# A recommendation-layer kernel on one core: x W as the first of ten equal passes, x*x times q as the last, two groups without the seven-product scheme, and the sums of x on VectorE

## The chip, the core and the metric

One NeuronCore of a Trainium2 chip runs the kernel. Its engines work in parallel, each through its own instruction list in order: TensorE (PE; PEld is its weight load), VectorE (DVE), ScalarE (ACT), GpSimd (POOL), and SyncE (SP), which here issues every DMA. Semaphores tie them together. The metric is device time in microseconds (us), less is better. The kernel before takes 815.57 us, the median of three runs (814.37 to 816.1).

## What is computed

```python
# x (2048, 512), beta (1024, 8, 512), W (1024, 512), b (1024)
s   = einsum('bn,hln->bhl', x, beta)
ssq = einsum('bn,hln->bhl', x * x, beta * beta)
y   = 0.5 * sum(s * s - ssq, axis=-1) + x @ W.T + b      # (2048, 1024), float32
```

Since the sum over l can be taken first, the part with ssq is (x*x) times q, with q[n, h] = -0.5 * sum over l of beta squared. So there are three products with the 512 columns n as inner dimension: x beta (8192 columns), x W (1024 columns) and (x*x) q (1024 columns).

## The kernel before

**Groups and passes.** The 2048 rows of x are cut into 8 pairs of 2 x 128 rows. The 8192 columns of beta are cut into 8 passes of 2 x 512 columns. A group is one pair in one pass: a 2 x 2 block product whose inner dimension is cut in two halves of 256 (two steps k of 128). It is done with seven block products instead of eight (Strassen and Winograd's scheme): the sums S1 to S4 of blocks of x, the sums T1 to T4 of blocks of beta, and seven sums behind the products. Each product is made in split single precision: a high part (a cast to fp32r) and a low part (the rest), and three matmuls high*high, high*low, low*high for each k. So a group is 7 x 2 x 3 = 42 matmuls of 128 x 128 by 128 x 512, and 64 groups are 2688.

**Who does what in a group g of the main passes.** PE writes the seven products into four PSUM banks (A, B, E, D; two sets in turn). ACT copies three first products out (`r1`, `r7`, `r5`, lines 549 to 563), and squares the results (lines 543, 569, 573). DVE adds r2 (L750), c12 (L729) and c21 (L721) and sums each eight squares (L738, two per group). POOL adds r5 + r7 (L902) and c22 (L909). The sums over l are stored to `fm_kept` in HBM by SP. The blocks of beta of the next pass are prepared meanwhile in seven steps: T sums on POOL, casts on ACT (L488), the low parts on DVE (L658), beta squared on ACT and its sum over l on DVE (L667, for q).

**The blocks of x.** In pass 0 SP loads each pair, POOL makes the sums S1 to S4 (lines 853 to 861), ACT casts the seven blocks (L538), DVE makes the low parts (L707), SP stores both to HBM. Later passes load them from there; four pairs have room in SBUF.

**The start.** Groups 0 and 1 are made together, product by product, in the order in which their operands come.

**The end.** After the 64 groups come 8 linear groups of 84 matmuls: x W and (x*x) q are added up in the same banks. x*x is made on DVE (L713) and q's blocks are loaded again from HBM, summed, cast and split between the last main group and the first linear one. Each linear group loads `fm_kept`, halves it and adds the bias (L823), adds the products on DVE and POOL, and stores the output. In all PE makes 2688 + 672 = 3360 matmuls, beside 10 to warm up.

The order of the work is written out by hand: every engine has one list, and nothing reorders it.

Of the kernel before, what the change touches and what calls it, by code (L numbers as in the profile page):

```python
# [31 lines left out]

W_PASS, Q_PASS = PASSES, PASSES + 1
SPLIT_FIRST = [B11, B21, T1, T3, B22, T2, T4]
SPLIT_LATER = [T3, B11, T1, B22, T2, B21, T4]
SPLIT_Q = [B11, T1, T3, T2, B21, B22, T4]
SUM_ORDER = [T3, T1, T2, T4]
SUM_ORDER_Q = [T1, T2, T3, T4]


def pairs_of(number):

    if number % 2 == 0:
# [12 lines left out]


def squares_in(i):

    return {1: [0], 2: [1, 2], 3: [3]}.get(i, [])  # L60


def t_split_place(c, op, k=KP - 1):

    if c == 0:
        return 1 + k if op == B11 else SPLIT_FIRST.index(op) + 2
    if c == Q_PASS:
        return 8 + OPS * (c - 1) + SPLIT_Q.index(op) + 1
    return 8 + OPS * (c - 1) + SPLIT_LATER.index(op) + 1


def t_sum_place(c, op):

    if c == 0:
        return {T2: 1, T4: 2}[op]
    return 2 + 4 * (c - 1) + (SUM_ORDER_Q if c == Q_PASS else SUM_ORDER).index(op) + 1


def s_split_place(p, rest=True):

    if p < 2:
        return p + (3 if rest else 1)
    return p + 3


def group_before(g):

    return {1: 0, 2: 1}.get(g, g)


def slot_of(l):

    return (3, 0) if l % 2 == 0 else (2, 1)


def fm_layer(nc, x_p, beta_p, w_p, bias, out):
# [10 lines left out]
    fm_kept = nc.dram_tensor("fm_kept", [B, H], f32, kind="Internal").ap()  # L107

    with ExitStack() as ctx:
# [7 lines left out]
        with ExitStack() as early:  # L117
            def early_sb(name, shape):
                return early.enter_context(nc.sbuf_tensor(name, shape, f32))

            t_hi_in = early_sb("t_hi_in", [P, 2, OPS, KP, COLS])
            t_lo_in = early_sb("t_lo_in", [P, 2, OPS, KP, COLS])
            s_hi_in = early_sb("s_hi_in", [P, HALF, OPS, 256])
            s_lo_in = early_sb("s_lo_in", [P, HALF, OPS, 256])
# [28 lines left out]
        q_loaded = sem("q_loaded")  # L153
# [3 lines left out]
        fm_stored = sem("fm_stored")  # L157
        fm_loaded = [sem(f"fm_loaded{i}") for i in range(2)]
# [3 lines left out]
        x_scaled = sem("x_scaled")  # L162
# [46 lines left out]


        def r1(g):
            return q_in[:, 0, 0, :] if g == 1 else r1_main[:, :]

        def r2(g):
            return q_in[:, 1, 0, :] if g == 1 else r2_main[:, :]

        def r5(g):
            return q_in[:, 2, 0, :] if g == 1 else r5_main[:, :]

        def r7(g):  # L220
            return q_in[:, 3, 0, :] if g == 1 else r7_main[:, :]

        def x_at(p):

            if p < 2:
                return s_hi_in[:, HALF - 1 - p, :, :]
            return s_lo_in[:, p % HALF if p < PAIRS else slot_of(p - PAIRS)[1], :, :]

        def x_loads(p):

            return 16 * (p // HALF + (p % HALF >= 2)) if p < PAIRS else 16 * (2 + (p - PAIRS) // 2)

        def t_at(c, op):

            if c == 0:
                return ub[:, :, :] if op == T1 else t_hi_in[:, 1, op, :, :]
            if c == Q_PASS and op in (B11, B21, B22):
                return q_in[:, op, :, :]
            return t_lo_in[:, c % 2, op, :, :]

        def f_at(l):
            if l % 2 == 0:
                return sq[:, :, :, :].rearrange("p r c h -> p r (c h)")
            return q_in[:, 0:2, :, :].rearrange("p r c h -> p r (c h)")

        @block.sync
        def _(sp):
            def load_first(op, k, loaded):

                ks = slice(0, KP) if k is None else slice(k, k + 1)  # L250
                sp.dma_start(t_hi_in[:, 1, op, ks, :], beta_p[0][:, op, ks, :]).then_inc(loaded, 16)

            def load_blocks(c):
                source = w_p if c == W_PASS else beta_p[c]
                sp.dma_start(t_lo_in[:, c % 2, 0:2, :, :], source[:, 0:2, :, :]).then_inc(right_loaded, 16)
                sp.dma_start(t_lo_in[:, c % 2, 2:4, :, :], source[:, 2:4, :, :]).then_inc(left_loaded, 16)
# [731 lines left out]
```

## Time and profile before

| | |
|---|---|
| median of 3 runs | 815.57 us |
| the profiled execution | 816.8 us, span 813.8 us |
| PE busy | 777.9 us (96%), 3370 matmuls |
| DVE, ACT, POOL busy | 509.9 us (63%), 386.2 us (47%), 410.5 us (50%) |
| moved by DMA | 134.81 MB, mean 166 GB/s |

The profile is of one execution. The span runs from its first to its last instruction, and the time of the execution is 3.0 us longer. Matmuls are pipelined: each is shown longer than the step from one to the next, so the busy share of PE says little, and the count of matmuls in a stretch says how fast it went.

### The profile page before, as it was taken

The numbers are of one execution on the slowest core, as the hardware profiler recorded it, in microseconds if no ns is written. First come the engines' busy times: TensorE is split into PE (matmuls) and PEld (weight loads), VectorE is DVE, ScalarE is ACT, GpSimd is POOL, SyncE is SP. The second block draws the span as 40 slices with busy tenths as digits, with TensorE's granted clock in tenths as the row PEclk, the third lists the DMA queues.
The fourth block names the chain that finished last, engine by engine and source line by source line (L and its number), as shares of the span: only waits on it lengthen the run. The fifth ranks groups of instructions, "written<-read, shape, count | busy, mean of one in ns | idle before, by whom it ended". The sixth has DMA issues, their size and how long they took to land. (4 is left out here: it accounts for less than half of the span.)

```text
span 813.8 us, 9328 instructions
## 1 busy us (share of the span) xinstructions
PE 777.9 (96%) x3370; PEld 633.8 (78%) x3370; DVE 509.9 (63%) x500; ACT 386.2 (47%) x530; POOL 410.5 (50%) x274
## 2 busy tenths in 40 slices
PE   6786889999999999999999999999999989999998
PEld 3664678888888888888888888888888768888886
DVE  5785695666566566657665666666555797654551
ACT  4465565555555455555554555555445552111110
POOL 5857645442632354344325442632454459866663
PEclk9799899999999999999999999999999999999999
DMA  8373526622650465065306622650476117666671
GB/s 335 155 250 138 213 104 229 208 88 73 250 194 14 136 205 184 13 217 198 104 16 230 216 76 87 236 194 13 140 305 235 39 46 270 233 220 220 220 263 59
DMA packets 44156, 134.81 MB, mean 166 GB/s; under 512 B 3536, under 2 KB 24016, under 8 KB 41936
## 3 DMA queue, kind: packets, MB, share of 16 engines
q1 hardware_dynamic: 44112, 134.23, 46.9%
q8 instruction: 26, 0.43, 0.2%
q14 instruction: 18, 0.15, 0.1%
HBM read 100.66 MB, written 33.55 MB: 165 GB/s over the span
## 5 line engine op out<-in xcount | busy, mean ns | idle before, releaser
L386 PE MATMUL bank<-t_hi,s_hi 128*128 128x512 f32 x1120 | 439.6, 392 | 26.0 <-DVE s_lo L707 17.8
L390 PE MATMUL bank<-t_lo,s_hi 128*128 128x512 f32 x1120 | 438.7, 392 | 4.8 <-DVE t_lo L658 4.8
L392 PE MATMUL bank<-t_hi,s_lo 128*128 128x512 f32 x1120 | 437.6, 391 | 0.0
L386 PEld LDWEIGHTS bank<-t_hi,s_hi 128*128 128x128 f32 x1120 | 211.4, 189 | 77.0 <-DVE s_lo L707 20.9
L390 PEld LDWEIGHTS bank<-t_lo,s_hi 128*128 128x128 f32 x1120 | 211.4, 189 | 51.4 <-DVE t_lo L658 8.2
L902 POOL TENSOR_TENSOR r<-r 128x512 f32<-128x512 f32 x71 | 103.4, 1456 | 283.6 <-ACT r L563 269.5
L392 PEld LDWEIGHTS bank<-t_hi,s_lo 128*128 128x128 f32 x1120 | 211.4, 189 | 43.9
L738 DVE TENSOR_REDUCE sums<-sq 128x128 f32<-128x1024 f32 x128 | 155.1, 1214 | 9.8 <-ACT sq L543 5.8
L729 DVE TENSOR_TENSOR sq<-bank,r 128x512 f32<-128x512 f32 x63 | 43.5, 690 | 110.2 <-PE bank L392 110.0
L750 DVE TENSOR_TENSOR r<-bank,r 128x512 f32<-128x512 f32 x71 | 49.0, 690 | 77.0 <-PE bank L392 73.5
L569 ACT ACTIVATE sq<-bank 128x512 f32<-128x512 f32 x64 | 38.3, 599 | 118.6 <-PE bank L392 118.6
L909 POOL TENSOR_TENSOR sq<-r 128x512 f32<-128x512 f32 x63 | 84.5, 1341 | 16.9 <-POOL r L902 6.9
L543 ACT ACTIVATE sq<-sq 128x1024 f32<-128x1024 f32 x64 | 68.0, 1062 | 42.0 <-DVE sq L721 35.5
L549 ACT COPY r<-bank 128x512 f32<-128x512 f32 x71 | 40.5, 570 | 87.3 <-PE bank L392 87.3
L658 DVE TENSOR_TENSOR t_lo<-t_lo_in,t_hi 128x1024 fp32r<-128x1024 f32 x60 | 79.6, 1329 | 0.0
L721 DVE TENSOR_TENSOR sq<-bank,r 128x512 f32<-128x512 f32 x63 | 43.5, 690 | 36.9 <-PE bank L392 36.8
L563 ACT COPY r<-bank 128x512 f32<-128x512 f32 x71 | 41.7, 588 | 49.5 <-PE bank L392 49.5
L488 ACT CAST t_hi<-t_lo_in 128x1024 fp32r<-128x1024 f32 x60 | 62.4, 1040 | 4.6 <-POOL t_lo_in L869 4.6
L555 ACT COPY r<-bank 128x512 f32<-128x512 f32 x71 | 41.7, 587 | 35.1 <-PE bank L392 35.1
L573 ACT ACTIVATE sq<-sq 128x512 f32<-128x512 f32 x64 | 40.5, 632 | 35.9 <-DVE sq L729 35.9
L853 POOL TENSOR_TENSOR s_lo_in<-s_lo_in 128x256 f32<-128x256 f32 x14 | 17.3, 1237 | 58.2 <-DVE s_lo_in L713 40.3
L707 DVE TENSOR_TENSOR s_lo<-s_lo_in,s_hi 128x1792 fp32r<-128x1792 f32 x14 | 37.1, 2647 | 12.4 <-ACT s_hi L538 12.4
(64 smaller groups left out, 408.1 us busy)
## 6 DMA issues: line engine op xcount, KB each, us to landing
s_hi<-s_hi_kept SPq DMA_DIRECT2D x34, 896.0 KB, 5.2
s_lo<-s_lo_kept SPq DMA_DIRECT2D x34, 896.0 KB, 7.5
t_lo_in<-beta_p SPq DMA_DIRECT2D x14, 1024.0 KB, 7.6
fm_kept<-sums SPq DMA_DIRECT2D x64, 128.0 KB, 1.8
s_lo_in<-x_p SPq DMA_DIRECT2D x14, 512.0 KB, 3.6
s_hi_kept<-s_hi SPq DMA_DIRECT2D x8, 896.0 KB, 3.6
s_lo_kept<-s_lo SPq DMA_DIRECT2D x8, 896.0 KB, 6.3
sq<-fm_kept SPq DMA_DIRECT2D x4, 1024.0 KB, 4.9
```

Source lines behind the costliest of these rows:

```text
L386: nc.tensor.matmul(to, s_hi[:, slot, s_op, cols], t_hi[:, t_slot, t_op, k, :], start=start, stop=False, skip_group_check=True)
L390: nc.tensor.matmul(to, s_hi[:, slot, s_op, cols], t_lo[:, t_slot, t_op, k, :], start=False, stop=False, skip_group_check=True)
L392: return nc.tensor.matmul(to, s_lo[:, slot, s_op, cols], t_hi[:, t_slot, t_op, k, :], start=False, stop=stop, skip_group_check=True)
L488: nc.scalar.copy(t_hi[:, c % 2, op, ks, :], t_at(c, op)[:, ks, :]).then_inc(t_hi_ready, 1)
L543: nc.scalar.activation(sq[:, 1, :, :], sq[:, 1, :, :], ACT.Square).then_inc(sq2_done, 1)
L658: nc.vector.tensor_tensor(t_lo[:, c % 2, op, ks, :], t_at(c, op)[:, ks, :], as_f32(t_hi[:, c % 2, op, ks, :]), ALU.subtract).then_inc(t_lo ...
L721: nc.vector.tensor_tensor(sq[:, 1, 0, :], bank(g, BANK_D), r2(g), ALU.add).then_inc(c21_added, 1)
L729: nc.vector.tensor_tensor(sq[:, 0, 1, :], bank(g, BANK_E), r2(g), ALU.add).then_inc(c12_added, 1)
L738: nc.vector.tensor_reduce(sums[:, row, :].rearrange("p (c h) -> p c h", c=2), sq[:, row, :, :].rearrange("p c (h l) -> p c h l", l=L), AX_ ...
L750: nc.vector.tensor_tensor(r2(g), bank(g, BANK_B), r1(g), ALU.add).then_inc(r2_added, 1)
L902: nc.gpsimd.tensor_tensor(r5(g), r5(g), r7(g), ALU.add).then_inc(r57_added, 1)
L909: nc.gpsimd.tensor_tensor(sq[:, 1, 1, :], r5(g), r2(g), ALU.add).then_inc(c22_added, 1)
```

## The change

There are now ten passes of eight groups, all of 42 matmuls, but for two groups.

- Pass 0 is x W. Its results, not squared, are stored to HBM as `acc_kept` (2048 x 1024), 1 MB per group.
- Passes 1 to 8 are those of beta. For each group SP loads its part of `acc_kept` (128 KB), POOL adds the bias, DVE adds half of the sum of squares (L785), SP stores it back.
- Pass 9 is (x*x) q, with q scaled by -0.5 and stored as the passes go. Its blocks are prepared in the steps of pass 8, as those of any other pass. x*x is made on ACT (`square_x`). The output is `acc_kept` plus the product.
- Groups 0 and 1 (`DIRECT`) are made with all eight block products, 48 matmuls each, from blocks of x and W without sums.
- The sums S1 to S4 are made on DVE, two groups ahead (`sum_s`), no longer on POOL. The pairs of groups 0 and 1 get theirs in pass 1 (groups 14 and 15).
- PE makes the products of a group in the order A, B, E, D, and then the second ones of A, E, D. The squares have two sets of buffers (`cs`). In pass 0 these hold results until the store of the group two before has landed (`wait_cs_free`).
- In pass 9, DVE adds r2, E's and D's first products itself (L853, L856), and PE waits for these sums where it waited for copies.

PE makes 96 + 78 x 42 = 3372 matmuls, beside the 10. The core of the diff, in the order tables, SyncE, PE, ACT, DVE, POOL:

```diff
+W_PASS, Q_PASS = 0, CHUNKS + 1
+FIRST_MAIN, FIRST_Q = PAIRS, PAIRS * Q_PASS
+GROUPS = PAIRS * (Q_PASS + 1)
+DIRECT = 2
+PREPARED = [2, 3, 4, 5, 6, 7, PAIRS + 6, PAIRS + 7] + list(range(FIRST_Q, GROUPS))
...
+        def wait_cs_free(engine, g, row):
+            if g < FIRST_MAIN + 2:
+                engine.wait_ge(v_stored[g % 2], 32 * (g // 2))
+            else:
+                engine.wait_ge(row1_summed if row == 0 else row2_summed, g - FIRST_MAIN - 1)
...
+            def load_acc(g):
+                m = g - FIRST_MAIN
...
+                if m >= 2:
+                    sp.wait_ge(acc_stored[g % 2], 16 * (m // 2))
+                sp.dma_start(acc[:, g % 2, :, :], acc_part(g)).then_inc(acc_loaded[g % 2], 16)
...
+            pe.wait_ge(s_lo_ready, 1)
+            whole(0, BANK_A, A11, B11, True)
+            pe.wait_ge(s_lo_ready, 2)
+            whole(0, BANK_D, A21, B11, True)
+            pe.wait_ge(s_lo_ready, 3)
+            whole(1, BANK_A, A11, B11, True)
+            whole(1, BANK_D, A21, B11, True)
+            for g in range(DIRECT):
+                whole(g, BANK_A, A12, B21, False).then_inc(direct_made, 1)
+                whole(g, BANK_D, A22, B21, False).then_inc(direct_made, 1)
...
+                if g < FIRST_Q:
+                    pe.wait_ge(r5_copied, count(g))
+                else:
+                    pe.wait_ge(r25_added, g - FIRST_Q + 1)
+                whole(g, BANK_E, S4, B22, False).then_inc(p3_made, 1)
...
+            for g in range(DIRECT, FIRST_Q):
+                copy_r1(g)
+                if g > FIRST_MAIN:
+                    square_row2(g - 1)
                 copy_r5(g)
                 copy_r7(g)
+                if g + 2 >= FIRST_Q:
+                    square_x(g + 2)
+                take_c11(g)
+                for s in steps_in(g):
+                    step(g // PAIRS + 1, s)
+                if g + 2 in PREPARED:
+                    split_s(g + 2)
...
+            for g in range(DIRECT, FIRST_Q + 1):
+                if g > DIRECT:
+                    add_c21(g - 1)
+                if g > FIRST_MAIN:
+                    sum_rows(g - 1)
...
+                if g + 1 in PREPARED:
+                    split_s(g + 1)
                 add_r2(g)
+                if g + 2 in PREPARED:
+                    sum_s(g + 2)
                 add_c12(g)
...
+                    pool.wait_ge(acc_loaded[g % 2], 16 * (m // 2 + 1))
+                    part = bias_all[:, (n - 1) * CHUNK_H:n * CHUNK_H]
+                    for row in range(2):
+                        made = nc.gpsimd.tensor_tensor(acc[:, g % 2, row, :], acc[:, g % 2, row, :], part, ALU.add)
+                    made.then_inc(acc_biased, 1)
+                pool.wait_ge(r5_copied, count(g))
+                pool.wait_ge(r7_copied, count(g))
```

VectorE at the start, before. `s_lo` are the low parts of x, `t_lo` those of beta (or of W), L753 makes T1 and T3, L750 is the first r2:

```order
L707 TENSOR_TENSOR s_lo<-s_hi_in,s_hi 128x512
L658 TENSOR_TENSOR t_lo<-t_hi_in,t_hi 128x512 x2
L707 TENSOR_TENSOR s_lo<-s_hi_in,s_hi 128x512
L658 TENSOR_TENSOR t_lo<-t_hi_in,t_hi 128x1024
L753 TENSOR_TENSOR ub<-t_hi_in 128x1024
L658 TENSOR_TENSOR t_lo<-ub,t_hi 128x1024
L707 TENSOR_TENSOR s_lo<-s_hi_in,s_hi 128x1280
L753 TENSOR_TENSOR t_hi_in<-t_hi_in 128x1024
L707 TENSOR_TENSOR s_lo<-s_hi_in,s_hi 128x1280
L658 TENSOR_TENSOR t_lo<-t_hi_in,t_hi 128x1024 x4
L750 TENSOR_TENSOR r<-bank,r 128x512
```

VectorE at the start, now. L741 splits x of groups 0 and 1, L745 makes T3, T1, T2 and T4, L724 to L731 the sums of group 2's x, L736 its low parts:

```order
L741 TENSOR_TENSOR s_lo<-s_lo_in,s_hi 128x1024
L675 TENSOR_TENSOR t_lo<-t_hi_in,t_hi 128x1024
L803 TENSOR_TENSOR t_lo<-t_hi_in,t_lo 128x1024
L675 TENSOR_TENSOR t_lo<-t_hi_in,t_hi 128x1024
L745 TENSOR_TENSOR t_hi_in<-t_hi_in 128x1024 x3
L675 TENSOR_TENSOR t_lo<-t_hi_in,t_hi 128x1024
L745 TENSOR_TENSOR t_hi_in<-t_hi_in 128x1024
L675 TENSOR_TENSOR t_lo<-t_hi_in,t_hi 128x1024 x2
L724 TENSOR_TENSOR s_lo_in<-s_lo_in 128x256
```

The four sums of T stand on VectorE now, and those of x behind them; the blocks without sums (the first four rows) come first, and PE's first 96 matmuls need no others.

SyncE behind the first loads, before: stores of the split x, then a load of x, once per group.

```order
L262 DMA s_hi_kept<-s_hi 128x1792
L264 DMA s_lo_kept<-s_lo 128x1792
L289 DMA s_lo_in<-x_p 128x1024
L283 DMA fm_kept<-sums 128x2x128
L262 DMA s_hi_kept<-s_hi 128x1792
```

SyncE behind the first loads, now, from the store of group 2's split x to the load of group 6's x:

```order
L271 DMA s_hi_kept<-s_hi 128x1792
L273 DMA s_lo_kept<-s_lo 128x1792
L261 DMA s_lo_in<-x_p 128x2x512 x2
L297 DMA acc_kept<-cs 128x1024
L304 DMA acc_kept<-cs 128x1024
L297 DMA acc_kept<-cs 128x1024
L304 DMA acc_kept<-cs 128x1024
L271 DMA s_hi_kept<-s_hi 128x1792
L273 DMA s_lo_kept<-s_lo 128x1792
L261 DMA s_lo_in<-x_p 128x2x512
```

The stores of 1 MB of results per group stand between those of x.

VectorE where the main groups end, before: from the sums of the last group but one to the first r2 of the linear groups.

```order
L729 TENSOR_TENSOR sq<-bank,r 128x512
L658 TENSOR_TENSOR t_lo<-q_in,t_hi 128x1024
L721 TENSOR_TENSOR sq<-bank,r 128x512
L658 TENSOR_TENSOR t_lo<-t_lo_in,t_hi 128x1024 x2
L738 TENSOR_REDUCE sums<-sq 128x128
L658 TENSOR_TENSOR t_lo<-t_lo_in,t_hi 128x1024
L738 TENSOR_REDUCE sums<-sq 128x128
L658 TENSOR_TENSOR t_lo<-t_lo_in,t_hi 128x1024
L658 TENSOR_TENSOR t_lo<-q_in,t_hi 128x1024 x2
L658 TENSOR_TENSOR t_lo<-t_lo_in,t_hi 128x1024
```

VectorE where the main groups end, now: c12 and c21 of group 71, its sums, the last split of q's blocks, x of group 73, and then r2 of group 72 and the two sums for which PE waits (L853, L856):

```order
L763 TENSOR_TENSOR cs<-bank,r 128x512
L769 TENSOR_TENSOR cs<-bank,r 128x512
L779 TENSOR_REDUCE sums<-cs 128x128 x2
L785 SCALAR_TENSOR_TENSOR acc<-sums,acc 128x256
L675 TENSOR_TENSOR t_lo<-t_lo_in,t_hi 128x1024
L736 TENSOR_TENSOR s_lo<-s_lo_in,s_hi 128x1792
L757 TENSOR_TENSOR r<-bank,r 128x512
L853 TENSOR_TENSOR r<-bank,r 128x512
L856 TENSOR_TENSOR r<-bank,r 128x512
```

Eight splits of blocks stood there, and one stands there now; the others are in the steps of pass 8.

## Rows read from the trace of the kernel before

**Rows 1.** The page: span, and TensorE's granted clock in 40 slices.
```profile
span 813.8 us, 9328 instructions
...
PEclk9799899999999999999999999999999999999999
```

**Rows 2.** Windows by stage: length, then busy us (x count) of each engine, clock, DMA.
```profile
0.00:110.00 110.00, 82.59 (x311) 59.83 (x312) 76.22 (x66) 60.63 (x75) 73.75 (x56) 0.92 0.56 206
110.00:640.00 530.00, 530.00 (x2340) 438.99 (x2339) 332.17 (x354) 284.17 (x406) 220.91 (x141) 1.00 0.44 153
640.00:670.00 30.00, 25.35 (x107) 19.36 (x106) 27.20 (x19) 17.63 (x22) 18.30 (x9) 1.00 0.07 17
670.00:810.00 140.00, 139.94 (x618) 115.58 (x616) 73.70 (x63) 23.73 (x28) 97.58 (x68) 1.00 0.61 216
```

**Rows 3.** Waits of PE: what for, us in total, times, the longest.
```profile
PE bank L386 <- DVE s_lo L707: 17.8, 7, 6.6
PE bank L386 <- ACT r L549: 7.9, 6, 2.0
```

**Rows 4.** Timeline of PE: start, us, instruction, idle before and its releaser.
```profile
5.75 0.47 PE L386 MATMUL bank<-t_hi,s_hi 128*128 128x512 f32 x1 [0.23 <-ACT t_hi L488]
...
18.07 0.50 PE L386 MATMUL bank<-t_hi,s_hi 128*128 128x512 f32 x1 [3.26 <-DVE s_lo L707]
...
108.48 0.50 PE L386 MATMUL bank<-t_hi,s_hi 128*128 128x512 f32 x1 [2.31 <-DVE s_lo L707]
...
809.55 0.39 PE L392 MATMUL bank<-t_hi,s_lo 128*128 128x512 f32 x1
```

**Rows 5.** Groups by line and shape: count, busy us, mean ns, idle before.
```profile
L738 DVE TENSOR_REDUCE sums<-sq 128x128 f32<-128x1024 f32 x128 | 155.1, 1214 | 9.8 <-ACT sq L543 5.8 <-issue 3.1 <-ACT sq L573 0.6
L902 POOL TENSOR_TENSOR r<-r 128x512 f32<-128x512 f32 x71 | 103.4, 1456 | 283.6 <-ACT r L563 269.5 <-ACT r L555 14.0
L658 DVE TENSOR_TENSOR t_lo<-t_lo_in,t_hi 128x1024 fp32r<-128x1024 f32 x60 | 79.6, 1329 | 0.0
L543 ACT ACTIVATE sq<-sq 128x1024 f32<-128x1024 f32 x64 | 68.0, 1062 | 42.0 <-DVE sq L721 35.5 <-POOL sq L909 6.4
L750 DVE TENSOR_TENSOR r<-bank,r 128x512 f32<-128x512 f32 x71 | 49.0, 690 | 77.0 <-PE bank L392 73.5
L563 ACT COPY r<-bank 128x512 f32<-128x512 f32 x71 | 41.7, 588 | 49.5 <-PE bank L392 49.5
L538 ACT CAST s_hi<-s_lo_in 128x1792 fp32r<-128x1792 f32 x14 | 23.9, 1705 | 16.8 <-POOL s_lo_in L861 16.8
L853 POOL TENSOR_TENSOR s_lo_in<-s_lo_in 128x256 f32<-128x256 f32 x14 | 17.3, 1237 | 58.2 <-DVE s_lo_in L713 40.3 <-DMA s_lo_in<-x_p 17.9
```

**Rows 6.** Timeline at the start: the first uses of the fifth and sixth load.
```profile
9.35 1.05 ACT L488 CAST t_hi<-t_hi_in 128x1024 fp32r<-128x1024 f32 x1 [1.42 <-DMA t_hi_in<-beta_p]
...
10.12 0.72 POOL L853 TENSOR_TENSOR s_hi_in<-s_hi_in 128x256 f32<-128x256 f32 x1 [9.68 <-DMA s_hi_in<-x_p]
```

**Rows 7.** Windows of loads alone, of stores, and of a low clock (columns as above).
```profile
10.00:15.00 5.00, 3.76 (x14) 2.17 (x12) 3.45 (x3) 2.43 (x4) 4.80 (x5) 1.00 1.05 426
45.00:50.00 5.00, 3.02 (x14) 2.26 (x13) 3.68 (x5) 4.92 (x7) 0.61 (x1) 1.00 1.00 337
...
82.20:86.70 4.50, 4.50 (x11) 3.53 (x12) 4.34 (x5) 2.24 (x3) 1.08 (x1) 0.50 0.85 336
```

**Rows 8.** Timeline: stores of split x issued, and first use of the x behind them.
```profile
43.02 0.41 SPq L262 DMA_DIRECT2D s_hi_kept<-s_hi  x1
...
51.23 1.21 POOL L853 TENSOR_TENSOR s_lo_in<-s_lo_in 128x256 f32<-128x256 f32 x1 [5.62 <-DMA s_lo_in<-x_p]
```

**Rows 9.** Timeline of VectorE: the same split of x, at two places.
```profile
80.14 2.01 DVE L707 TENSOR_TENSOR s_lo<-s_lo_in,s_hi 128x1792 fp32r<-128x1792 f32 x1
...
707.47 3.09 DVE L707 TENSOR_TENSOR s_lo<-s_lo_in,s_hi 128x1792 fp32r<-128x1792 f32 x1 [0.17 <-ACT s_hi L538]
```

**Rows 10.** Timeline of SyncE's queue: the last store.
```profile
810.74 0.33 SPq L304 DMA_DIRECT2D out<-q_in  x1
```

More of the change, by code:

```diff
@@ L86, in group_before, with pair_of, slot_of, count @@
[L86 to L93, printed above, removed]
+def pair_of(g):
+    return order_of(g // PAIRS)[g % PAIRS]
+def slot_of(g):
+    return pair_of(g) % HALF
+def count(g):
+    return g - DIRECT + 1
+def steps_in(g):
+    n, i = g // PAIRS, g % PAIRS
+    if n == 0:
+        return {2: [1], 3: [2], 4: [3, 4], 5: [5], 6: [6], 7: [7]}.get(i, [])
+    return [i] if i and n < Q_PASS else []
+def t_split_place(n, op, k=KP - 1):
+    if n == 0:
+        return {B11: 1 + k, B21: 3, B22: 5, T1: 6, T2: 7, T3: 8, T4: 9}[op]
+    return FIRST_SPLITS + OPS * (n - 1) + SPLIT_ORDER.index(op) + 1
@@ L229, in x_loads, with x_at @@
[L229 to L244, printed above, removed]
+        def x_at(g):
+            return s_lo_in[:, slot_of(g), :, :]
@@ L315, in _ @@
+            load_x_part(0, 0, x0_front_loaded)
+            load_first(B11, b11_loaded[0], slice(0, 1))
+            load_first(B11, b11_loaded[1], slice(1, 2))
+            load_x_part(0, 1, x0_rest_loaded)
+            load_x_part(1, 0, x1_loaded)
+            load_x_part(1, 1, x1_loaded)
+            load_first(B21, b21_loaded)
+            load_first(B12, b12_loaded)
+            load_first(B22, b22_loaded)
             load_x(2)
@@ new lines, in _ @@
+            for g in range(FIRST_Q, GROUPS):
+                i = g - FIRST_Q
+                if i <= HALF:
+                    sp.wait_ge(p4_made, count(g - 1))
+                    load_x(g + HALF - 1)
+                if i == 0:
+                    load_f(0)
+                    load_f(1)
+                    store_acc(FIRST_Q - 1)
+                    for other in range(2, 6):
+                        load_f(other)
+                if 1 <= i <= 2:
+                    load_f(5 + i)
+                if i:
+                    store_rows(g - 1)
@@ L398, in whole @@
                 for k in range(KP):
-                    ready = t_split_place(c, t_op, k) if g % PAIRS == 0 else None
-                    made = product(bank(g, place), slot, s_op, c % 2, t_op, k,
-                                   start and k == 0, stop and k == KP - 1, ready)
-                return made
-            for g in range(2):
-                pe.wait_ge(s_hi_ready, s_split_place(g, False))
-                pe.wait_ge(s_lo_ready, s_split_place(g, False))
-                whole(g, g, BANK_A, A11, B11, True, True).then_inc(p1_made, 1)
@@ new lines, in _, with wait_bank @@
+            for g in range(DIRECT):
+                whole(g, BANK_E, A12, B22, False).then_inc(direct_made, 1)
+                whole(g, BANK_B, A22, B22, False).then_inc(direct_made, 1)
+            def wait_bank(g, place):
+                before = g - 2
+                if before < DIRECT:
+                    pe.wait_ge(direct_copied, {BANK_A: 1, BANK_D: 2, BANK_E: 5, BANK_B: 6}[place] + 2 * before)
+                elif place == BANK_A and before >= FIRST_Q:
+                    pe.wait_ge(o11_added, before - FIRST_Q + 1)
+                else:
+                    pe.wait_ge({BANK_A: c11_taken, BANK_B: r2_added, BANK_E: c12_added,
+                                BANK_D: c21_added}[place], count(before))
@@ L652, in _ @@
+            for g in range(FIRST_Q, GROUPS):
+                copy_r1(g)
+                if g == FIRST_Q:
+                    square_row2(g - 1)
+                if g + 2 < GROUPS:
+                    square_x(g + 2)
+                    split_s(g + 2)
         @block.vector
@@ new lines, in add_o21 @@
+            def add_o21(g):
+                i = g - FIRST_Q
+                dve.wait_ge(p4_made, count(g))
+                dve.wait_ge(f21_added, i + 1)
+                f = f_at(i)
+                nc.vector.tensor_tensor(f[:, 1, 0:COLS], bank(g, BANK_D), f[:, 1, 0:COLS], ALU.add
+                                        ).then_inc(c21_added, 1)
+            split_x(0, slice(0, 2), 1)
+            for k in range(KP):
+                split_low(0, B11, slice(k, k + 1))
+            split_x(0, slice(2, 4), 2)
@@ L803, in _ @@
[L803 to L829 removed]
+            split_s(2)
```

1127 lines of the change are left out of this document (490 added, 637 removed).

## The prediction

> **What bounds the kernel now.** I read the page first [rows 1]: the span is 813.8 us, and TensorE's clock was low in two places only, both in the first tenth. Then the windows by stage [rows 2]. Between 110 and 640 us they count 2340 matmuls in 530 us, 0.2266 us each, at full clock (2.4 GHz), and PE is never idle. So the main stage goes at PE's own pace, and no edit to another engine's work makes it shorter. What can be won is outside it. The first 110 us hold 311 matmuls, 10 of them to warm up. The first real one starts at 5.75 and the last at 809.55 [rows 4]. 110 - 5.75 - 301 x 0.2266 = 36.0 us are lost there. Between 640 and 670 it is 30 - 107 x 0.2266 = 5.8 us. The linear groups from 670 on lose nothing. Behind the last matmul 813.8 - 809.55 = 4.25 us go by. The sum: 5.75 + 3359 x 0.2266 (761.1) + 36.0 + 5.8 + 4.25 = 812.9, which is 0.9 short of the span, so I call the whole loss 42.7. The waits of PE say whose they are [rows 3]: the low parts of x (L707), up to 6.6 us at once, behind POOL's sums, and the copies of ACT, which stand behind its wait for the same sums. A low clock adds to it: the window of 4.5 us at 0.50 holds 11 matmuls [rows 7], where 20 would fit at 0.2266, so a fall costs 4.5 - 11 x 0.2266 = 2.0 us.
>
> **The frame of the new time.** 3372 - 3360 = 12 matmuls more cost 2.7 us. The first is unchanged (same two first loads), 5.75. The tail holds one VectorE add and a store as before [rows 10]: the last store is half as large, but 0.8 MB go out just ahead of it in the same queue, so I leave it at 4.25 (between 3.7 and 4.6). 5.75 + 3371 x 0.2266 (763.9) + 4.25 = 773.9, plus what PE loses. Now the losses, stage by stage.
>
> **Groups 0 and 1: 3.2 us.** PE needs no sums there, only splits. The fifth load of before has 1.6 MB up to its end and is used at 9.35, the sixth (1.8 MB) at 10.12 [rows 6]; from there 426 GB/s [rows 7]. In the new order 1.6 MB reach to both halves of x of group 1 (9.3), then B21 10.8, B12 12.0, B22 13.3. ACT casts 1024 columns in 1.05; VectorE splits 512 in 0.69 and 1024 in 1.22 (the mean of 1.33 [rows 5] holds two long ones; 2 x 0.69 less one start gives the same). So x of group 1 is ready at 9.3 + 1.05 + 1.2 = 11.6, and PE, which has 12 matmuls before it, waits about 1.6 us. Then 12 matmuls until 14.4, and B21 is ready at 13.1, B12 at 14.4, B22 at 15.6: the other 72 run on, until 30.7. Lost: 30.7 - 5.75 - 96 x 0.2266 = 3.2. No gap there is near the 3.26 us after which the clock fell [rows 4]; if it falls, 2.0 more.
>
> **Group 2: 0.** VectorE from 15.6 on: three sums of T and T1's low part 4 x 1.2 = 20.4, T4's sum and two low parts 24.0, the sums of x, T4's low part, split. A sum of 256 columns has no row on VectorE. 0.69 for 512 and 1.22 for 1024 give 0.53 per 512, so 0.69 - 0.27 = 0.43. Bounds: 0.27, without the fixed part, and 0.74, POOL's undisturbed (its mean is 1.24 [rows 5]). Four are 1.7: 25.7, T4 26.9, ACT's cast (1.7) until 27.4, the split 2.0 [rows 9]: 29.5. PE wants it at 30.7, so 1.2 are spare. With 0.74 each it is still in time; with late loads it costs up to 2.
>
> **Groups 3 to 7: 1.6 us.** SP issues in a row two stores of group 2's x (1.84 MB, 29.6), two loads (1.05), and the results of groups 0 and 1 (1.05 each). Stores ran at 337 GB/s [rows 7]. In the old kernel 2.36 MB from 43.02 were used at 51.23, 8.2 us [rows 8], which is 7.0 for the bytes and 1.2 besides. So the results of group 0 have landed at 29.6 + 3.94/0.337 + 1.2 = 42.5. ACT's `take_c11(2)` needs that buffer and would run at 37.5: it waits 5 us, and behind it on ACT stand the square of beta, a cast of T3 (together 2.0) and the cast of group 4's x (1.7), then `copy_r1(3)`: 42.5 + 0.6 + 2.0 + 1.7 + 0.6 = 47.4. PE wants it in group 3 after 24 matmuls, at 40.2 + 5.4 = 45.7. Lost 1.6 to 1.7. If the queue drains at 426 it is 0; at 250, 5. Later groups ask for 1.84 + 1.05 MB in 9.5 us, 304 GB/s, under 337, and are in time. VectorE's fullest group there (c21, T1 and B22 with a sum of squares, split, r2, sums, c12) takes 0.7 + 3.6 + 2.0 + 0.7 + 1.7 + 0.7 = 9.4 of 9.5.
>
> **Pass 1: 1.0 us.** GpSimd now waits for a load of `acc` before r5 + r7; behind it on POOL is c22, and ACT's squares, `copy_r5` of the next group and r2 wait for that. For group 8 the load stands behind 2.1 MB of beta and 1.05 MB of results, and lands 11 us into the group; the bias takes 1.0, r5 + r7 1.5 [rows 5], c22 as much, 15 in all, and `copy_r5(9)` is ready just when PE asks. 0, at worst 2. In groups 13 to 15 VectorE carries everything at once: c21 0.7, two reductions 2.4 [rows 5], acc 0.45, sum and split 2.4, the split of x 2.0, r2 0.7, sums 1.7, c12 0.7: 11.1 against 9.5. So the split for group 15 ends about 1 us after PE wants it (0 to 3).
>
> **Passes 1 to 8 otherwise: 0.** VectorE, busy for 332 of 530 us [rows 2], gets 0.45 more per group of 9.5, POOL two adds of 128 columns (under 0.74 each). The load of `acc` waits in SP for the store of two groups before, and lands about 3 us into its group; c22 may come 8 us later before PE notices.
>
> **Into pass 9: 3.5 + 2.0 us.** This takes the place of the old 5.8. Counted from the start of group 72, VectorE has c12 and c21 of group 71 until 1.6; its row 2 waits for ACT (cast of x 73 until 2.1, square 0.6, copy 0.59, row 2 1.06 [rows 5]), so reductions and acc end at 5.8, the T4 split at 7.0, x 73 at 8.9, r2 at 9.5, and r5's sum at 10.3. PE waits for that sum after 30 matmuls, at 6.8: 3.5 lost (1 to 5). The copies on ACT did not stand behind all this. An idle time of 2.31 left the clock at 1.00, one of 3.26 was followed by 0.50 [rows 1, 4], so I count a fall, 2.0. In the rest of pass 9 VectorE has 6 x 0.69 + 2.0 + 1.7 = 7.9 of 9.5 us: nothing lost.
>
> One rule is weighed here. The split of x took 2.01 at one place and 3.09 at another, where POOL added beside it [rows 9]. The Trainium skill (SBUF — State Buffer, "SBUF: two separate sides") says that a VectorE instruction with two SBUF inputs and a GpSimd one lock each other out for a whole instruction. By that, the split for group 15 could wait for one r5 + r7 more, 1.3 to 1.5 us, and 787 would be 788; the trace shows 1.1 more.
>
> **The sum.** 3.2 + 0 + 1.6 + 1.0 + 3.5 + 2.0 = 11.3; 773.9 + 11.3 = 785.2 span. The profiled execution took 816.8, 3.0 more than its span, and 1.2 more than the median: 785.2 + 3.0 - 1.2 = 787.0, 3.5% less than 815.57. Its own range is 783 to 792.
>
> **Rivals.**
> - Nothing is late: the queue drains faster, the clock stays up, VectorE's chain into pass 9 costs 1 to 2. Loss 4 to 6, time 780 to 782. For it: the loads at 426 GB/s. Against it: 337 with stores.
> - The start is late by more: stores at 250, the clock falls at the start and again in group 3 or 9, VectorE's 256-column sums at 0.74 (1.2 more per group in groups 2 to 7, where only 0.1 is spare). Loss 18 to 24, time 794 to 800. For it: clock falls and 5 us idle times are what the old start has.
> - Slower than before: the loop load, add, store of `acc` is late in each of the 63 groups that wait on it. POOL would then make c22 late, ACT's `copy_r5`, and PE. It decides once a load lands more than 11 us into its group; each 0.5 us beyond that costs 31 us, 818. Against it: 8 us to spare by the rates above.
> - The change doesn't do what it says: if PE's stalls at the start are those of the loads and not of POOL's sums, the loss of 36 stays and only the end moves, 815. Against it: PE's releasers [rows 3], and 1.8 MB landed by 10.12 while the waits go on to 108 [rows 4].
>
> **How the numbers follow.** Forecast 0.5, nothing late 0.22, later start 0.22, slower 0.04, no change 0.02. A measurement tells about 0.2% (1.6 us) from no change. Faster is the first three, 0.94; same 0.02, slower 0.04. The range takes in both neighbours: 779 to 798.
>
> **What would show it.** Right: about 135 matmuls done by 40 us and none of PE's waits on x in groups 0 to 2; ACT's copy of A in group 2 waiting for a store until 42; PE waiting near group 72 for L853 on VectorE some 3.5 us. Wrong: PE idle in the main passes, or GpSimd's bias add (L906) ended by a DMA just before PE's waits.

## The result, and the profile after

The changed kernel takes 802.44 us (median of 4 runs, 801.89 to 804.58), beside 815.26 us of the kernel before on the same chip: ratio 0.9848, 95% interval 0.9827 to 0.9869. It is 1.5% faster, where 3.5% was forecast, and 802.4 is outside the range 779 to 798. The profiled execution took 802.24 us, its span is 800.5.

The page of after, beside [rows 1]: the span, and TensorE's granted clock, low now in one late slice instead of two early ones.

```profile
span 800.5 us, 9817 instructions
...
PEclk9999999999999999999999999999999999998999
```

Windows by stage, beside [rows 2]; the columns are the same (length, then PE, PEld, DVE, ACT, POOL, clock, DMA share, GB/s):

```profile
0.00:110.00 110.00, 102.29 (x430) 79.67 (x430) 77.18 (x80) 54.72 (x71) 32.34 (x25) 1.00 0.74 282
110.00:160.00 50.00, 45.90 (x192) 37.13 (x193) 41.95 (x45) 26.85 (x38) 28.49 (x26) 0.97 0.38 122
160.00:640.00 480.00, 478.39 (x2111) 395.90 (x2110) 322.91 (x375) 266.95 (x381) 244.27 (x224) 1.00 0.46 158
640.00:700.00 60.00, 60.00 (x266) 49.73 (x265) 36.99 (x45) 30.53 (x46) 32.84 (x29) 1.00 0.56 195
700.00:730.00 30.00, 23.75 (x94) 18.56 (x94) 27.01 (x32) 13.18 (x17) 9.73 (x9) 0.89 0.61 221
```

430 matmuls stand in the first 110 us where 311 stood. A matmul at full clock takes a step of 0.2267 us to the next. So 110 to 160 has lost 50 - 192 x 0.2267 = 6.5 us, and 700 to 730 has lost 30 - 94 x 0.2267 = 8.7, at mean clocks of 0.97 and 0.89. The one wait inside 160 to 640 is that of group 15. PE's waits, beside [rows 3]:

```profile
PE bank L432 <- DVE s_lo L736: 6.6, 4, 3.4
PE bank L432 <- DVE r L853: 5.5, 1, 5.5
PE bank L432 <- ACT r L579: 4.2, 5, 1.8
...
PE bank L432 <- DVE s_lo L741: 1.0, 2, 0.8
PE bank L432 <- ACT r L585: 0.8, 1, 0.8
```

The timeline of PE, beside [rows 4]: the first matmul, the two longest idle times (groups 14 and 72), the last matmul.

```profile
5.07 0.77 PE L432 MATMUL bank<-t_hi,s_hi 128*128 128x512 f32 x1
...
155.58 0.78 PE L432 MATMUL bank<-t_hi,s_hi 128*128 128x512 f32 x1 [3.36 <-DVE s_lo L736]
...
725.18 0.80 PE L432 MATMUL bank<-t_hi,s_hi 128*128 128x512 f32 x1 [5.47 <-DVE r L853]
...
796.24 0.39 PE L438 MATMUL bank<-t_hi,s_lo 128*128 128x512 f32 x1
```

The steps between matmuls over 0.2267 us, added up group by group, give PE's losses. 5.07 + 3371 x 0.2267 (764.2) + 27.0 + 4.26 behind the last matmul = 800.5, the span.

| groups | forecast | after |
|---|---|---|
| 0 and 1 | 3.2 | 3.0 |
| 2 | 0 | 0 |
| 3 to 7 | 1.6 | 6.3 (1.45, 1.13, 2.38, 1.35, 0) |
| 9 | 0 (0 to 2) | 1.1 |
| 13 to 15 | 1.0 (0 to 3) | 7.75 (0.59, 5.23, 1.93) |
| 72, with a fall of the clock | 5.5 | 8.9 |
| sum | 11.3 | 27.0 |

So PE lost 15.7 us more than forecast, nearly all of it where VectorE sums and splits x. The same lines by form, beside [rows 5], show which durations were off:

```profile
L736 DVE TENSOR_TENSOR s_lo<-s_lo_in,s_hi 128x1792 fp32r<-128x1792 f32 x16 | 35.4, 2211 | 5.8 <-ACT s_hi L558 5.8
...
L725 DVE TENSOR_TENSOR s_lo_in<-s_lo_in 128x256 f32<-128x256 f32 x16 | 15.4, 962 | 0.0
L728 DVE TENSOR_TENSOR s_lo_in<-s_lo_in 128x256 f32<-128x256 f32 x16 | 13.5, 842 | 0.0
L724 DVE TENSOR_TENSOR s_lo_in<-s_lo_in 128x256 f32<-128x256 f32 x16 | 12.4, 774 | 3.1 <-DMA s_lo_in<-x_p 2.4 <-ACT s_lo_in L565 0.7
...
L731 DVE TENSOR_TENSOR s_lo_in<-s_lo_in 128x256 f32<-128x256 f32 x16 | 7.1, 442 | 0.6
```

I had priced a sum of 256 columns at 0.43. The fourth one (L731) takes 0.44, the other three 0.77 to 0.96 in the mean. The timeline of group 3 says why. VectorE:

```profile
48.52 0.68 DVE L757 TENSOR_TENSOR r<-bank,r 128x512 f32<-128x512 f32 x1
49.12 0.92 DVE L724 TENSOR_TENSOR s_lo_in<-s_lo_in 128x256 f32<-128x256 f32 x1
49.96 1.51 DVE L725 TENSOR_TENSOR s_lo_in<-s_lo_in 128x256 f32<-128x256 f32 x1
51.39 2.61 DVE L728 TENSOR_TENSOR s_lo_in<-s_lo_in 128x256 f32<-128x256 f32 x1
54.04 0.42 DVE L731 TENSOR_TENSOR s_lo_in<-s_lo_in 128x256 f32<-128x256 f32 x1
```

And GpSimd beside it:

```profile
47.14 2.61 POOL L910 TENSOR_TENSOR r<-r 128x512 f32<-128x512 f32 x1 [1.56 <-ACT r L591]
49.83 1.36 POOL L914 TENSOR_TENSOR cs<-r 128x512 f32<-128x512 f32 x1
51.15 2.58 POOL L873 TENSOR_TENSOR t_lo_in<-t_lo_in 128x1024 f32<-128x1024 f32 x1
```

Each long sum ends 0.3 us behind a GpSimd operation: 49.96 + 1.51 = 51.47 behind c22 (51.19), 51.39 + 2.61 = 54.00 behind T's sum (53.73). The first sum (49.12 + 0.92 = 50.04) ends as far behind r5 + r7 (L910, 49.75). So a sum is not slowed, it waits until the other is through. Four sums take 5.3 us (49.12 to 54.46) instead of 1.7. The order of the lists brings this about: the sums of x stand behind r2 (L757) on VectorE, c22 on GpSimd waits for r2 and for r5 + r7, and T's sum stands behind c22. So GpSimd's operations run while those on x do. How many of the four sums meet one differs: three of the set shown, two of the set for group 6 (from 61.48 on), one of the set for group 7 (from 74.48 on).

VectorE ahead of the two longest waits: the sums of x and the add into `acc` for group 14, then the split and a sum just ahead of group 72's wait.

```profile
138.91 1.48 DVE L724 TENSOR_TENSOR s_lo_in<-s_lo_in 128x256 f32<-128x256 f32 x1
140.30 1.52 DVE L725 TENSOR_TENSOR s_lo_in<-s_lo_in 128x256 f32<-128x256 f32 x1
141.75 2.62 DVE L728 TENSOR_TENSOR s_lo_in<-s_lo_in 128x256 f32<-128x256 f32 x1
144.40 0.57 DVE L731 TENSOR_TENSOR s_lo_in<-s_lo_in 128x256 f32<-128x256 f32 x1
...
149.95 1.39 DVE L785 SCALAR_TENSOR_TENSOR acc<-sums,acc 128x256 f32<-128x256 f32 x1
...
708.98 3.13 DVE L736 TENSOR_TENSOR s_lo<-s_lo_in,s_hi 128x1792 fp32r<-128x1792 f32 x1
...
712.97 1.51 DVE L725 TENSOR_TENSOR s_lo_in<-s_lo_in 128x256 f32<-128x256 f32 x1
```

GpSimd runs beside each of these: T's sum from 141.50 to 144.08 beside the third, for one.

### The profile page after: what moved, and what is told of

Read it like the earlier page. It is cut to its first block and busy times, and to the rows that moved or that the text cites. A ratio compares the mean times of both kernels' runs of the same rounds, so it can differ in the third digit from the quotient of the medians.

```text
span 800.5 us, 9817 instructions
## 1 busy us (share of the span) xinstructions
PE 776.9 (97%) x3382; PEld 635.8 (79%) x3382; DVE 557.1 (70%) x642; ACT 410.4 (51%) x564; POOL 374.2 (47%) x332
## 5 line engine op out<-in xcount | busy, mean ns | idle before, releaser
L910 POOL TENSOR_TENSOR r<-r 128x512 f32<-128x512 f32 x70 | 107.7, 1538 | 226.3 <-ACT r L591 226.3
L779 DVE TENSOR_REDUCE sums<-cs 128x128 f32<-128x1024 f32 x128 | 155.5, 1215 | 76.6 <-ACT cs L610 71.8
L763 DVE TENSOR_TENSOR cs<-bank,r 128x512 f32<-128x512 f32 x70 | 48.3, 691 | 90.7 <-PE bank L438 87.9
L914 POOL TENSOR_TENSOR cs<-r 128x512 f32<-128x512 f32 x70 | 91.1, 1301 | 27.4 <-issue 18.3
L873 POOL TENSOR_TENSOR t_lo_in<-t_lo_in 128x1024 f32<-128x1024 f32 x36 | 87.1, 2421 | 30.0 <-PE bank L438 29.7
L906 POOL TENSOR_TENSOR acc<-acc,bias_all 128x128 f32<-128x128 f32 x128 | 60.3, 492 | 86.5 <-DMA acc<-acc_kept 86.4
L579 ACT COPY r<-bank 128x512 f32<-128x512 f32 x78 | 45.8, 587 | 84.4 <-PE bank L438 84.4
L675 DVE TENSOR_TENSOR t_lo<-t_lo_in,t_hi 128x1024 fp32r<-128x1024 f32 x63 | 79.5, 1262 | 0.0
L585 ACT COPY r<-bank 128x512 f32<-128x512 f32 x70 | 41.2, 588 | 73.8 <-PE bank L438 73.8
L769 DVE TENSOR_TENSOR cs<-bank,r 128x512 f32<-128x512 f32 x70 | 48.3, 690 | 40.3 <-PE bank L438 40.3
L610 ACT ACTIVATE cs<-cs 128x1024 f32<-128x1024 f32 x64 | 68.0, 1062 | 4.6 <-POOL cs L914 4.6
L558 ACT CAST s_hi<-s_lo_in 128x1792 fp32r<-128x1792 f32 x16 | 27.2, 1700 | 77.9 <-DVE s_lo_in L731 77.9
L591 ACT COPY r<-bank 128x512 f32<-128x512 f32 x70 | 41.3, 589 | 48.6 <-PE bank L438 48.6
L599 ACT ACTIVATE cs<-bank 128x512 f32<-128x512 f32 x64 | 38.4, 600 | 46.1 <-PE bank L438 46.1
L757 DVE TENSOR_TENSOR r<-bank,r 128x512 f32<-128x512 f32 x78 | 53.2, 683 | 2.9 <-PE bank L438 2.9
```

The source lines that it names most:

```text
L610: nc.scalar.activation(cs[:, g % 2, 1, :, :], cs[:, g % 2, 1, :, :], ACT.Square).then_inc(sq2_done, 1)
L675: nc.vector.tensor_tensor(t_lo[:, n % 2, op, ks, :], t_at(n, op)[:, ks, :], as_f32(t_hi[:, n % 2, op, ks, :]), ALU.subtract).then_inc(t_lo ...
L757: nc.vector.tensor_tensor(r2[:, :], bank(g, BANK_B), r1[:, :], ALU.add).then_inc(r2_added, 1)
L779: nc.vector.tensor_reduce(sums[:, row, :].rearrange("p (c h) -> p c h", c=2), cs[:, g % 2, row, :, :].rearrange("p c (h l) -> p c h l", l= ...
L873: nc.gpsimd.tensor_tensor(t_at(n, op), t_at(n, left), t_at(n, right), ALU.subtract).then_inc(t_summed, 1)
L906: made = nc.gpsimd.tensor_tensor(acc[:, g % 2, row, :], acc[:, g % 2, row, :], part, ALU.add)
```

## The experiments

**1. GpSimd short.** GpSimd's adds in groups 2 to 79, except the sums of T, work on 8 columns; so most of r5 + r7, of c22, of the biases and of the output is left out. ACT squares r5 in place of c22.

```diff
-nc.gpsimd.tensor_tensor(cs[:, g % 2, 1, 1, :], r5[:, :], r2[:, :], ALU.add).then_inc(c22_added, 1)
+nc.gpsimd.tensor_tensor(cs[:, g % 2, 1, 1, 0:8], r5[:, 0:8], r2[:, 0:8], ALU.add).then_inc(c22_added, 1)
```

> The changed kernel, with the adds of GpSimd behind the products (r5 + r7, c22, the bias, the three output adds) made of 8 columns and not of 512 or 128; the T sums stay whole, ScalarE squares r5 as it is, so this part of the result is left out. DVE, DMA and PE have the same amount of work. Theory A (a VectorE add with two inputs in SBUF and a GpSimd add lock each other out, so that sums of x that take 0.42 us alone take 1.5 and 2.6 us behind c22 and a T sum): what PE loses falls from 27 us to 14 to 19, time 790 to 795; the L725 sums fall to 0.42, those of L724 or L725 that meet a T sum stay at 2 or more. Theory B (VectorE simply has too much to do in these groups) and theory C (the stores of results hold buffers too long): nothing changes but the few tenths by which c22 is earlier, 800 to 803.

Measured: 788.02 us (787.03 to 788.61), ratio to before 0.9657 (0.9631 to 0.9684). PE loses 13.2 us in its trace: 2.9 in groups 0 and 1, 1.65 in group 3, 1.2 and 1.1 in groups 14 and 15, 6.1 in group 72, whose wait is now 3.57. That is 1.9 more than the sum of 11.3 that I had made, and near it term by term: with these adds of GpSimd short, the forecast nearly holds. (The time is below the 790 to 795 expected.) The sums of T were left whole, and beside them a sum of x still took 2.62, three times in groups 2 to 15: the run takes most of the collisions away, not all. The exclusion, called the lock from here on, works in the other direction too. This add has 8 columns, and takes 1.51 us beside a split of x:

```profile
47.25 1.51 POOL L912 TENSOR_TENSOR r<-r 128x8 f32<-128x8 f32 x1 [1.56 <-ACT r L593]
49.43 0.26 POOL L916 TENSOR_TENSOR cs<-r 128x8 f32<-128x8 f32 x1 [0.67 <-POOL r L912]
```

```profile
46.69 2.01 DVE L738 TENSOR_TENSOR s_lo<-s_lo_in,s_hi 128x1792 fp32r<-128x1792 f32 x1
```

It ends at 48.76, just behind the split (48.70). Alone, adds of 8 columns on this line take 0.20.

**2. The sums of x on GpSimd**, all else as after:

```diff
-                nc.vector.tensor_tensor(at[:, S1, :], at[:, A21, :], at[:, A22, :], ALU.add).then_inc(s_summed, 1)
+                nc.gpsimd.tensor_tensor(at[:, S1, :], at[:, A21, :], at[:, A22, :], ALU.add).then_inc(s_summed, 1)
```

> The changed kernel with the sums of x back on GpSimd, still two groups ahead, at the head of its list for the group. Theory A: GpSimd is in order, so its own sums can't collide with its c22 and T sums; VectorE is freed of 3 to 5 us in groups 2 to 7, 12, 13 and from 70 on, GpSimd gets 3 to 7 us more where 4 to 5 are free. PE's wait of 5.5 us before group 72's E product falls to about 3, the losses in groups 13 to 15 to 3; time 792 to 800. Theory B: the same side, since VectorE has less to do, 790 to 798. Theory C: no change, 800 to 803. That GpSimd becomes the bound: above 803, with ScalarE's cast of x waiting for it.

Measured: 798.66 us (797.56 to 800.16), ratio 0.979 (0.9761 to 0.9819), 3.8 us less than after. Groups 4 and 5 lose nothing and 15 almost nothing, group 14 1.4; but group 3 loses 4.5, groups 6 and 9 1.7 and 1.4, and group 72 11.0. There the sums of x stand ahead of c22 on GpSimd:

```profile
703.94 1.46 POOL L855 TENSOR_TENSOR s_lo_in<-s_lo_in 128x256 f32<-128x256 f32 x1 [3.15 <-ACT s_lo_in L565]
705.35 2.52 POOL L856 TENSOR_TENSOR s_lo_in<-s_lo_in 128x256 f32<-128x256 f32 x1
707.83 0.73 POOL L859 TENSOR_TENSOR s_lo_in<-s_lo_in 128x256 f32<-128x256 f32 x1
708.65 0.74 POOL L862 TENSOR_TENSOR s_lo_in<-s_lo_in 128x256 f32<-128x256 f32 x1
...
711.56 1.29 POOL L912 TENSOR_TENSOR cs<-r 128x512 f32<-128x512 f32 x1
```

A sum costs 0.73 here when alone, and 1.5 and 2.5 beside VectorE's splits of T and of x. So moving the sums moves the collision: the lock is paid on either engine.

**3. The sums ahead of r2**, in passes 0 to 8. No work is left out, only the order on VectorE changes:

```diff
-                add_r2(g)
                 if g + 2 in PREPARED:
                     sum_s(g + 2)
+                add_r2(g)
                 add_c12(g)
```

> The changed kernel with VectorE's sums of x for two groups ahead made before r2 and not behind it, in passes 0 to 8. Theory A: c22 on GpSimd waits for r2, so it can't run beside the sums any more, and the T sum behind c22 neither; the four sums take 1.7 to 3 us and not 4.9 (group 3), the losses of groups 3 to 15 fall from 15 to 5 to 9 us; time 792 to 797. Theory B: the amount of work is the same, so r2 is only later, 802 or more. Theory C: no change.

Measured: 791.21 us (790.95 to 791.72), ratio 0.9698 (0.9673 to 0.9724), just below the 792 to 797 expected. This is the strongest evidence for the lock, since GpSimd does all its work: run 1 took 13.8 us out of PE's losses, and order alone takes 10.9 (27.0 to 16.1). Added up over groups 2 to 15, VectorE's instructions took 20.7 us more in after than as many of the shortest of their line and shape; here this excess is 10.9. The edit also makes the sums earlier by the length of r2 (0.68), and no run separates the two effects. In group 4 the four sums take 58.58 to 61.22, with one collision (with r5 + r7) instead of two:

```profile
58.58 1.52 DVE L724 TENSOR_TENSOR s_lo_in<-s_lo_in 128x256 f32<-128x256 f32 x1
60.02 0.41 DVE L725 TENSOR_TENSOR s_lo_in<-s_lo_in 128x256 f32<-128x256 f32 x1
60.36 0.41 DVE L728 TENSOR_TENSOR s_lo_in<-s_lo_in 128x256 f32<-128x256 f32 x1
60.80 0.42 DVE L731 TENSOR_TENSOR s_lo_in<-s_lo_in 128x256 f32<-128x256 f32 x1
```

c22 waits for r2, so it can't start beside them.

**4. In pass 9 the split of x behind the sums that PE waits for** (order of after otherwise):

```diff
-                if g + 1 < GROUPS:
-                    split_s(g + 1)
                 add_r2(g)
...
                 nc.vector.tensor_tensor(r5[:, :], bank(g, BANK_D), r5[:, :], ALU.add).then_inc(r257_added, 1)
+                if g + 1 < GROUPS:
+                    split_s(g + 1)
```

> The changed kernel with the split of the next x behind the two sums for which PE waits, in pass 9. All theories: PE's wait in group 72 falls by the length of the split, 2.0 us, from 5.5 to 3.5; losses elsewhere stay; the clock may stay up then, 0 to 2 more. Time 798 to 800.5. If the wait doesn't fall, something other than VectorE's list order ends it.

Measured: 803.12 us (802.2 to 803.5), ratio 0.9845 (0.9814 to 0.9876): no gain, where 798 to 800.5 was expected. The wait at group 72 fell from 5.47 to 3.54, as it had to. But groups 75 to 79 each wait 0.3 us for the split and lose 0.6: 1.9 won once, 2.9 lost. Groups 2 to 71, whose order is that of after, lost 15.1 us in both traces, though not group by group: group 3 lost 4.0 here and 1.45 in after.

From here on each kernel has the order of run 3. Runs 5 to 8 were made on another chip than runs 1 to 4; the kernel before took 815.13 us on it, and 815.17 on the first.

**5. The row sums of group 71 behind r5 of group 72** on VectorE:

```diff
-                if g > FIRST_MAIN:
+                if FIRST_MAIN < g < FIRST_Q:
                     sum_rows(g - 1)
...
                 nc.vector.tensor_tensor(r5[:, :], bank(g, BANK_D), r5[:, :], ALU.add).then_inc(r257_added, 1)
+                if i == 0:
+                    sum_rows(g - 1)
```

> The kernel of the run before with sums ahead of r2 (791.2 us), and in it one change: the two row sums and the add into acc of the last group of beta (group 71) stand behind the sum r5 of group 72 on VectorE, no longer ahead of its r2. Theory A (PE's wait at group 72 is VectorE's list, in which 2 x 1.22 + 0.42 + small gaps = 3.3 us stand ahead of the sum of E that PE wants): the wait falls from 4.0 to about 0.7, the clock does not fall behind it, and the time is 4 to 5 us less, 786.5. Rival B (the wait is that of ACT's work for that group, the square of x, the cast and the squares of row 2): the wait stays at 4, time 791. Rival C (the split of x for group 73 is then late instead): VectorE is late by 1 to 2 at the start of group 73, time 788 to 789.

Measured: 787.62 us (787.43 to 787.75), ratio 0.9657 (0.9642 to 0.9671), 3.6 less than run 3. The wait fell from 4.01 to 0.62 with no fall of the clock behind it, and 0.91 came back in group 73, whose r2 is late in turn. That is a little less gain than forecast (4 to 5 us, 786.5); theory A stands, with 0.9 us of rival C in it.

**6. The results of group 0 stored first:**

```diff
-            store_s(2)
             sp.wait_ge(direct_made, 6)
             load_x(4)
+            store_v(0)
+            store_s(2)
             sp.wait_ge(direct_made, 8)
             load_x(5)
-            store_v(0)
```

> The kernel with sums ahead of r2 (791.2 us), and in SyncE's list the results of group 0 are stored ahead of the sums of group 2, and both behind the load of pair 4. Theory A (PE's wait of 1.7 us for the copy r1 in group 3 comes from ACT's copy of A in group 2, which waits until 41.5 us for the store of group 0's results, behind 1.84 MB of sums in the queue): that copy waits until 37 to 38 at most and PE's wait is gone, 2.0 us less, 789.3. Rival B (ACT's own casts in groups 2 and 3 make it late): the wait in group 3 stays over 1, time 791.

Measured: 788.29 us (787.23 to 788.67), ratio 0.9663 (0.9647 to 0.9679). PE's wait in group 3 is gone, and that in group 6 too, which I had not expected: 3.7 us less in groups 3 to 6. ACT in its trace, `take_c11(2)` first:

```profile
36.61 0.59 ACT L597 COPY cs<-bank 128x512 f32<-128x512 f32 x1 [0.77 <-PE bank L438]
...
40.69 0.59 ACT L579 COPY r<-bank 128x512 f32<-128x512 f32 x1
```

It waits only for PE now, and the copy r1 of group 3 starts at 40.69, where it started at 45.44 in after. Why the wait in group 6 went is not shown. The time is 1.0 us under the forecast's 789.3, and not 1.7 (3.7 less the 2.0 expected), since group 72 kept its wait of 4.04 and lost 6.6 with the clock's fall (5.8 in run 3).

**7. The split of x straight behind c21**, ahead of the row sums and of T's low parts:

```diff
+                if g + 1 in PREPARED and g < FIRST_Q:
+                    split_s(g + 1)
                 if g > FIRST_MAIN:
                     sum_rows(g - 1)
...
-                if g + 1 in PREPARED:
-                    split_s(g + 1)
```

> The kernel with sums ahead of r2 (791.2 us), and VectorE splits x for the next group straight behind c21, ahead of the row sums and of the low parts of T (3.3 to 4 us earlier). Its losses at the starts of groups 6, 14 and 15 are 1.7, 1.2 and 1.5 us, each ended by that split. Theory A (these are the order within the group: the split is the only one of VectorE's operations that PE wants at the group's end): all three go, r2 stays where it was, 786.5 to 787.5. Rival B (VectorE has more than 9.5 us of work in these groups, so what is late only changes its name): the losses come back as waits for r2 or the copy r1, 790 to 791. Rival C (the split now meets the T sum of GpSimd in groups 3 to 6, 2.0 becomes 3.1 and more): groups 4 to 6 lose 1 to 2 each, 790 to 793.

Measured: 785.9 us (785.46 to 788.62), ratio 0.9647 (0.9623 to 0.9671), a little below the 786.5 to 787.5 of theory A. The losses of groups 6, 14 and 15 are gone, and none came back under another name: those groups had time enough, and it was the order that cost it. There are still collisions (the T sum at 52.93 takes 4.18 on GpSimd), but what waits there is no longer what PE wants next.

**8. The changes of order of runs 3, 5, 6 and 7 together:**

> Sums ahead of r2, split straight behind c21, the row sums of group 71 behind r5 of group 72, the results of group 0 stored first. If the causes are those named, each its own, the gains add up: 791.2 - 4.5 - 2.0 - 4 = 780.5 to 782, with a loss of 4 to 6 us in all, most of it in groups 0 and 1 and in group 9. If one late step covers another (rival), it stays at 784 to 787.

Measured: 780.73 us, the median of four executions; three took 780.29 to 781.07, and one 1586, for which the trace, taken of another, gives no reason. The ratio, 0.9571 (0.9553 to 0.9588), leaves that one out. The expectation, 780.5 to 782, held. The kernel leaves nothing out, and its median is 34.4 us below that of the kernel before and 21.7 below that of the changed one. PE's waits in its trace:

```profile
...
PE bank L432 <- DVE r L853: 1.1, 1, 1.1
PE bank L432 <- DVE s_lo L741: 0.7, 1, 0.7
PE bank L432 <- ACT r L585: 0.5, 1, 0.5
PE bank L432 <- ACT t_hi L511: 0.4, 1, 0.4
```

It loses 5.8 us: 3.1 in groups 0 and 1, 0.8 in group 9, 1.4 in group 73. 5.08 + 764.2 + 5.8 + 4.25 = 779.3, its span.

## Why the prediction was wrong

**What held.** The frame: 5.75 + 763.9 + 4.25 against 5.07 + 764.2 + 4.26. Groups 0 to 2: 3.2 and 0 against 3.0 and 0, in part by luck: 1.0 was lost at x of group 1, where 1.6 was forecast, and nearly all the rest before it. The store in group 2: "42.5", measured 41.46 in the trace of after:

```profile
41.46 0.59 ACT L597 COPY cs<-bank 128x512 f32<-128x512 f32 x1 [5.44 <-DMA acc_kept<-cs]
```

and group 3 lost 1.45 to the 1.6 forecast; run 6 shows the cause. The main passes from group 16 on lose nothing, so the load of `acc` costs no time there and the rival with a slow `acc` loop is out. The bias of group 8, forecast to make r5 ready "just when PE asks", made it 0.8 us late in group 9. A VectorE list too long ahead of r5 in group 72 was forecast, and run 1 measures it alone at 3.57 (forecast 3.5); a fall of the clock came with it.

**The step that failed** is the price of VectorE's work on x beside GpSimd, which left out the wait for GpSimd's running instruction: "0.69 - 0.27 = 0.43" for a sum, "1.7" for four, 2.0 for a split. These are the undisturbed durations, and right as such: alone, the four took 0.42 each at 22.97 to 24.5. In the groups that count they took 0.4 to 2.6, and the split up to 3.1. Two other operations with two inputs in SBUF were priced the same way: T's low parts (L675), at 1.2, took up to 2.48, and the add into `acc` (L785), at 0.45, took 1.39 at 149.95 and at 164.07. From this came three terms:
- Groups 3 to 7, "9.4 of 9.5": with 0.1 to spare, 3.6 us more in group 3 could only come out as waits. 6.3 instead of 1.6.
- Groups 13 to 15, "11.1 against 9.5": the four sums of x for group 14 took 1.48, 1.52, 2.62 and 0.57. 7.75 instead of 1.0, with a fall of the clock behind the 3.36.
- Group 72: a sum and a split of x just ahead of it took 1.1 us more each (1.51 and 3.13), and the wait was 5.47 instead of 3.5.

The bounds failed with it. I bounded a sum by 0.27 and 0.74, both undisturbed durations, though [rows 9] held a collision of 1.1 us, and [rows 5] a mean of 1.24 for GpSimd's sum, of which [rows 6] shows one at 0.72. I wrote that mean down and priced the change without it.

**The rule.** I applied it to one split and one r5 + r7. The Trainium skill (SBUF — State Buffer, "SBUF: two separate sides") says that the loser is blocked for the whole instruction, and by that every VectorE operation with two SBUF inputs had to be laid beside GpSimd's list. The trace of after has up to three such pairs among the sums of x of one group, 0.5 to 2.2 us each. The trace agrees with the rule in each pair above, and in its limits too. In the trace of after, 61 of 70 c12 (L763), with one input from PSUM, overlapped an r5 + r7, c22 or sum of T on GpSimd, and none took over 0.69; 36 of the 128 row sums (L779), with one input, did, and none took over 1.22.

**The rivals.** The time fell between the rivals' values, nearest to the one with a later start (794 to 800, a loss of 18 to 24). That it came near is luck. Groups 0 to 9 lost 5.6 us more than forecast, and the other 10.1 lie in groups 13 to 15 and 72, which it didn't name. Its mechanism is wrong too: groups 0 to 2 are as forecast, the clock did not fall before group 14, and the sums at 0.74 would have cost 1.2 per group, not up to 3.6.

## What to carry to other kernels

Before work with two SBUF inputs is moved to VectorE, lay it beside GpSimd's list: an overlap cost up to 2.2 us here beside a GpSimd instruction of 2.58, and the same holds the other way round. Put it where GpSimd waits for something, ahead of the operation that releases GpSimd (experiment 3), and put first in each group what TensorE asks for next (experiments 5 and 7). The reorderings of run 8, without new work, won 21.7 us, more than the change itself had.

## What the runs showed of the hardware

- The lock holds to the end of the other instruction: an add of 8 columns, 0.20 us alone, took 1.51 beside a split of x, and ended 0.06 us behind it.
- TensorE's clock. Idle times of 1.81 us and less in the changed kernel and the eight runs were followed by a clock of 1.00; those of 2.06 (run 4, group 3), 2.62 (run 2, group 3) and 3.34 or more were followed by 0.50, that is 1.2 GHz. But one of 2.31 in the kernel before was not [rows 4]. So the length of the idle time alone doesn't decide; what else does stays open. In the 5 us behind the waits at group 72 with a fall, PE made 12 to 15 matmuls, where it makes 22. Over its whole length, a fall cost 1.6 to 3.0 us, the steps of about 0.427 us in place of 0.2267 added up.
- The windows of run 1 behind its wait of 3.57 (columns as in [rows 2]). 10 matmuls stand in the first 4 us, at a clock of 0.50, where 4 / 0.2267 = 17.6 would fit:

```profile
711.00:715.00 4.00, 4.00 (x10) 3.10 (x10) 3.09 (x7) 1.54 (x1) 0.20 (x1) 0.50 1.02 403
715.00:719.00 4.00, 4.00 (x16) 3.24 (x15) 2.64 (x3) 1.52 (x3) 0.00 (x0) 0.85 1.03 419
```
